# One loop step of a six-layer windowed-attention kernel, issued in another order: the transposes of a step stand together between the two halves of the scores

## The reference, cut to what matters

```python
for i in range(DEPTH):                     # 6
    x = attn_layer(shift_tokens(x), Wqkv[i], q_scale[i], k_scale[i], Wo[i]) + x
    x = ffn_layer(shift_tokens(x), ln_g[i], ln_b[i], W1[i], b1[i], W2[i], b2[i]) + x
# attn_layer: q, k, v = split(x @ Wqkv) in 16 heads of 64; q, k = l2norm, scale, rotary
#   (a rotary table times xPos scale); attention of each window of 32 tokens to itself and the
#   window before, softmax(8 * q k^T + mask) v; then @ Wo
# ffn_layer: layer norm, hg = xn @ W1 + b1 (2 x 341 wide), (a * gelu(gate)) @ W2 + b2
```

## Time and profile before

| | |
|---|---|
| median of 3 runs | 1505.93 us (1504.41 to 1509.35) |
| profiled execution | 1507.59 us, span of its trace 1505.8 us |
| busy, share of the span | TensorE 96%, VectorE 88%, ScalarE 77%, GpSimd 80% |
| chain that ended last | TensorE 89%, VectorE 5%, issue 2%, GpSimd 2% |

### The profile page before, as it was taken

One profiled execution on the slowest core, in us unless ns is written; L12 is line 12 of the kernel. 1 busy time (PEld: TensorE's weight loads), 2 busy tenths in 40 slices (PEclk: granted clock), 3 DMA queues, 4 the chain that ended last, 5 costly groups with the idle time before them and its releaser, 6 DMA issues.

```text
span 1505.8 us, 74802 instructions
## 1 busy us (share of the span) xinstructions
PE 1441.7 (96%) x32904; PEld 785.9 (52%) x32904; DVE 1327.1 (88%) x1789; ACT 1162.2 (77%) x2289; POOL 1209.8 (80%) x1051
## 2 busy tenths in 40 slices
PE   6877999999999999999999999999999999999985
PEld 6823444545545545545545545545555545545553
DVE  5478999989999989999999999989999999999974
ACT  4337888878888788888888888888888788888871
POOL 5148999878888888888888888888888888888841
PEclk9968999999999999999999999999999999999998
DMA  5100000020000020000020000020000000000000
GB/s 206 30 1 30 3 10 10 3 66 10 4 20 15 4 66 10 3 20 15 3 66 10 4 19 15 4 66 10 3 20 15 4 10 10 4 20 15 4 17 29
DMA packets 24564, 32.93 MB, mean 22 GB/s; under 512 B 2372, under 2 KB 21424, under 8 KB 23344
## 3 DMA queue, kind: packets, MB, share of 16 engines
q1 hardware_dynamic: 24240, 28.15, 5.8%
HBM read 20.80 MB, written 1.05 MB: 15 GB/s over the span
## 4 chain that ended last, share of the span: by engine, by line
PE 89%; DVE 5%; issue 2%; POOL 2%; ACT 1%; DMA 1%; SPq 0%; POOLq 0%; DVEq 0%; ACTq 0%
PE psq L257 22%; PE ring L279 21%; PE ring L309 11%; PE pss L298 9%; PE ring L267 9%; PE ring L323 8%; PE ring L333 4%; PE ring L346 1%; DVE qa L825 1%; PE ring L382 1%; DVE qb L841 1%; DVE mx L983 1%; DVE qb L961 1%; DMA xf<-x 0%; DMA mh<-in_bv 0%
## 5 line engine op out<-in xcount | busy, mean ns | idle before, releaser
L279 PE MATMUL ring<-mh,x0S 128*32 128x512 f32 x3072 | 407.9, 595 | 0.0
L257 PE MATMUL psq<-wqk,x0S 128*32 128x512 f32 x3072 | 394.9, 612 | 5.9 <-ACT sq L1200 4.9
L1332 POOL TENSOR_TENSOR qa<-qa,qb 128x1024 f32<-128x1024 f32 x96 | 229.2, 2388 | 6.7 <-DVE qb L961 6.7
L1391 POOL TENSOR_TENSOR qa<-qa,qb 128x1024 f32<-128x1024 f32 x96 | 228.6, 2382 | 0.0
L309 PEld LDWEIGHTS ring<-u,pT 128*32 128x32 f32 x6144 | 171.4, 111 | 61.8 <-issue 60.1
L309 PE MATMUL ring<-u,pT 128*32 128x128 f32 x6144 | 191.6, 274 | 4.1 <-DVE pT L978 4.1
L1373 POOL TENSOR_TENSOR pr<-pr,rden 128x1024 f32<-128x1024 f32 x96 | 183.9, 1916 | 12.8 <-DVE rden L860 12.8
L257 PEld LDWEIGHTS psq<-wqk,x0S 128*32 128x32 f32 x3072 | 93.6, 111 | 184.2 <-issue 168.4
L1352 POOL TENSOR_TENSOR qa<-qa,rn 128x1024 f32<-128x1024 f32 x96 | 182.7, 1903 | 0.2
L1368 POOL TENSOR_TENSOR qa<-qa,rn 128x1024 f32<-128x1024 f32 x96 | 182.8, 1904 | 0.0
L298 PEld LDWEIGHTS pss<-kT,qT 64*32 64x32 f32 x12288 | 134.8, 105 | 91.1 <-issue 83.6
(11 more groups left out here) (172 smaller groups left out, 2724.3 us busy)
## 6 DMA issues: line engine op xcount, KB each, us to landing
wqk<-in_wqk SPq DMA_DIRECT2D x6, 1024.0 KB, 8.6
mvT<-in_mvT SPq DMA_DIRECT2D x6, 512.0 KB, 3.8
wo<-in_wo SPq DMA_DIRECT2D x6, 512.0 KB, 5.2
xf<-x SPq DMA_DIRECT2D x24, 128.0 KB
xf<-x SPq DMA_DIRECT2D x24, 127.0 KB
rope<-in_rope SPq DMA_DIRECT2D x1, 2048.0 KB, 10.0
w<-in_w SPq DMA_DIRECT2D x6, 341.0 KB, 3.0
xmid<-in_x SPq DMA_DIRECT2D x4, 256.0 KB, 4.2
```

The lines of the kernel that those rows point to most:

```text
L257: last = mm(psq[WIN * w:WIN * w + WIN, 512 * (n % 2):512 * (n % 2) + 512], x0S[:, tile * P + WIN * w:tile * P + WIN * w + WIN], wqk[:, l % ...
L279: last = mm(bank[WIN * g:WIN * g + WIN, :], x0S[:, tile * P + WIN * w:tile * P + WIN * w + WIN], mh[:, l % 2, g, :, :].rearrange("p j n -> ...
L1332: g_.tensor_tensor(qa[:, t % 2, 1024:2048], qa[:, t % 2, 1024:2048], qb[:, 1024:2048], ALU.add).then_inc(sum_k, 1)
L1391: g_.tensor_tensor(qa[:, t % 2, 0:1024], qa[:, t % 2, 0:1024], qb[:, 0:1024], ALU.add).then_inc(sum_q, 1)
```

## The change

The instructions are the same, in number and form; each engine issues them in another order and with other lags.

TensorE after: H, Y part 1 (t=s-6), A2, A0, U1, U0 (s-4), K(s-1), S0(s-4), T01(s-3), T23(s-3), S1(s-4), U3(s-5), F, G0, U2(s-4), G1, A1, Z, Q(s-1), X, G2, Y part 0 (s-5). By s mod 4: F in 0; H, G0, G1 in 1; A0, A1, G2 in 2; A2, Z, X in 3.

VectorE after: L961, L983, L978, A1 (L834), statistics (L895), L816, Z (L929), L825, L841, Y (L851), L867, L956, L936, L969, A2 (L906), A0 (L876), L857, L860, L947. ScalarE after: T2 and T3 copies, L1124, U3, G0, L1157 to L1163, xh, U2, G2, X, F0, G1, F1, L1204, L1200, the exponential (L1176), U0, H, U1, L1254, L1129 and L1133, T0 and T1 copies. G0 and G1 stand ahead of the exponential of one step, G2 ahead of that of the next. GpSimd after: L1346, L1332, L1336, L1338, L1368, L1352, the group's norm, L1391, L1373, L1328. (Numbers are those of the lines before.) The chunks of the first part and the last group's norm move with them: the first K now stands in step 1 behind chunks 4, 5 and 6.

The diff of TensorE's loop, cut to the guards and the calls (waits and bank bookkeeping are left out and go with their calls):

```diff
@@ -506,89 +506,41 @@
+i = group_at(s, 9)
+        merge((j, j + 1), l)
-i = group_at(s, 14)
-    hidden(ring[bank], 2, 1).then_inc(filled[bank], 1)
-t = s - 5
-    values(ring[bank], t, 3).then_inc(filled[bank], 1)
-t = s - 4
-    values(ring[bank], t, 2).then_inc(filled[bank], 1)
-t = s - 4
-    scores(t, 1).then_inc(s_ready, 1)
-t = s - 3
-    turn([ring[bank] for bank, n in banks], t, 0)
-t = s - 1
-    project(t, 0)
-    project(t, 1).then_inc(pq_done, 1)
-i = group_at(s, 14)
-    hidden(ring[bank], 1, 0).then_inc(filled[bank], 1)
-i = group_at(s, 12)
-    halves_turned([ring[bank] for bank, n in banks], lambda blk: xh[:, blk * P:blk * P + P], QUAD)
-t = s - 5
-    mix(ring[bank], t, 0)
-i = group_at(s, 13)
-    hidden(ring[bank], 0, 1).then_inc(filled[bank], 1)
-u = unit_at(s, 3)
-t = s - 5
+t = s - 6
     mix(ring[bank], t, 1).then_inc(filled[bank], 1)
-i = group_at(s, 13)
+i = group_at(s, 15)
+    hidden(ring[bank], 2, 0).then_inc(filled[bank], 1)
+i = group_at(s, 14)
     hidden(ring[bank], 0, 0).then_inc(filled[bank], 1)
-t = s - 3
+t = s - 4
+    values(ring[bank], t, 1).then_inc(filled[bank], 1)
+t = s - 4
@@ -597,42 +549,7 @@
     values(ring[bank], t, 0).then_inc(filled[bank], 1)
-i = group_at(s, 15)
-    narrow(ring[bank]).then_inc(filled[bank], 1)
-i = group_at(s, 14)
-    hidden(ring[bank], 2, 0).then_inc(filled[bank], 1)
-t = s - 3
-    values(ring[bank], t, 1).then_inc(filled[bank], 1)
-i = group_at(s, 8)
-        merge((j, j + 1), l)
-i = group_at(s, 13)
-    hidden(ring[bank], 1, 1).then_inc(filled[bank], 1)
-t = s - 0
+t = s - 1
@@ -648,6 +565,94 @@
     project(t, 2)
     project(t, 3).then_inc(pk_done, 1)
+t = s - 4
+    scores(t, 0)
+t = s - 3
+    turn([ring[bank] for bank, n in banks], t, 8)
+t = s - 3
+    turn([ring[bank] for bank, n in banks], t, 0)
+t = s - 4
+    scores(t, 1).then_inc(s_ready, 1)
+t = s - 5
+    values(ring[bank], t, 3).then_inc(filled[bank], 1)
+u = unit_at(s, 3)
+i = group_at(s, 12)
+    halves_turned([ring[bank] for bank, n in banks], lambda blk: xh[:, blk * P:blk * P + P], QUAD)
+i = group_at(s, 13)
+    hidden(ring[bank], 0, 1).then_inc(filled[bank], 1)
+t = s - 4
+    values(ring[bank], t, 2).then_inc(filled[bank], 1)
+i = group_at(s, 13)
+    hidden(ring[bank], 1, 1).then_inc(filled[bank], 1)
+i = group_at(s, 14)
+    hidden(ring[bank], 1, 0).then_inc(filled[bank], 1)
+i = group_at(s, 15)
+    narrow(ring[bank]).then_inc(filled[bank], 1)
+t = s - 1
+    project(t, 0)
+    project(t, 1).then_inc(pq_done, 1)
 i = group_at(s, 15)
@@ -658,24 +663,19 @@
     halves_turned([ring[bank] for bank, n in banks], lambda blk: x0T[:, QUAD * (i % GROUPS) + blk, :], QUAD)
-t = s - 2
-    turn([ring[bank] for bank, n in banks], t, 8)
-t = s - 3
-    scores(t, 0)
+i = group_at(s, 14)
+    hidden(ring[bank], 2, 1).then_inc(filled[bank], 1)
+t = s - 5
+    mix(ring[bank], t, 0)
```

And of ScalarE's, the blocks around the gates and the exponential:

```diff
+                i = group_at(s, 13)
...
+                    nc.scalar.activation(uT[0:rows, 0, :], ring[bank][0:rows, :], ACT.Gelu,
...
+                i = group_at(s, 14)
...
+                    nc.scalar.activation(uT[0:rows, 2, :], ring[bank][0:rows, :], ACT.Gelu,
...
+                i = group_at(s, 13)
...
+                    nc.scalar.activation(uT[0:rows, 1, :], ring[bank][0:rows, :], ACT.Gelu,
...
+                t = s - 4
+                if 0 <= t < STEPS:
+                    act.wait_ge(p_shifted, t + 1)
+                    nc.scalar.activation(pr[:, t % 2, :], pr[:, t % 2, :], ACT.Exp, scale=QK_SCALE).then_inc(exp_done, 1)
```

More of the change, by code:

```diff
@@ L557, in _ @@
-                t = s - 5
[L558 to L563, removed]
-                    mix(ring[bank], t, 0)
-                i = group_at(s, 13)
[L566 to L570, removed]
-                    if i % GROUPS == 0:
-                        pe.wait_ge(w1_ready, 16 * (i // GROUPS + 1))
-                    wait(pe, freed[bank], n)
-                    hidden(ring[bank], 0, 1).then_inc(filled[bank], 1)
@@ L650, in _ @@
                     project(t, 3).then_inc(pk_done, 1)
+                t = s - 4
+                if 0 <= t < STEPS:
+                    if t == 0:
+                        mask(t)
+                    wait(pe, mask_ready, t)
+                    bank, n = place["T1", t]
+                    pe.wait_ge(freed[bank], n + 1)
+                    bank, n = place["T3", t]
+                    pe.wait_ge(freed[bank], n + 1)
+                    pe.wait_ge(kprev_ready, t + 1)
+                    scores(t, 0)
@@ new lines, in _ @@
+                if chunk_at(s - 1, 3) >= 0:
+                    chain_d(chunk_at(s - 1, 3))
+                i = group_at(s, 13)
+                if i >= 0:
+                    bank, n = take("G0", i)
+                    for r in range(2):
+                        nbank, m = place["F%d" % r, i]
+                        pe.wait_ge(freed[nbank], m + 1)
+                    if i % GROUPS == 0:
+                        pe.wait_ge(w1_ready, 16 * (i // GROUPS + 1))
+                    wait(pe, freed[bank], n)
+                    hidden(ring[bank], 0, 1).then_inc(filled[bank], 1)
@@ L826, in _ @@
                                     tab[:, t % 2, 0, :].unsqueeze(1).broadcast_to([P, HEADS, HD]), ALU.mult)
[L827 to L837 removed]
+                if chunk_at(s, 0) >= 0:
+                    chain_W(chunk_at(s, 0))
                 t = s - 1
@@ new lines, in _ @@
+                i = group_at(s, 8)
+                if 0 <= i < LASTG:
+                    l, first = i // GROUPS + 1, i % GROUPS
+                    for j in ((first, first + 1) if first % 2 == 0 else ()):
+                        bank, n = place["H%d" % j, l]
+                        act.wait_ge(filled[bank], n + 1)
+                        nc.scalar.copy(mh[:, l % 2, :, 2 * (j % 2) + j // 2, :],
+                                       ring[bank][:, :].rearrange("p (k n) -> p k n", k=4)).then_inc(freed[bank], 1)
```

699 lines of the change are left out of this document (337 added, 362 removed).

## The result

The kernel after takes 1521.17 us (median of 4 runs, 1519.28 to 1522.56), the kernel before beside it 1506.78 (4 runs): a ratio of 1.0094 with a 95% interval of 1.0074 to 1.0115. The change costs 14 us, where I had forecast 1508.2 with a range of 1490 to 1530. The profiled execution took 1520.87 us, its span is 1518.8, 13.0 above the span before.

What follows compares the result with a forecast made beforehand. TensorE's blocks from start to start were taken as the bound. Terms -24 (blocks), +5 (X alone), +19.3 (psq loop), +2 (start and end) gave +2.3 us: 1508.2 against a median of 1505.93, range 1490 to 1530.

Steps and rivals of the forecast that it cites:

- TensorE's blocks: TensorE's steps: leaving the wide tiling once instead of twice saves 0.25 us a step, -24 us over 96 steps.
- The rival in which nothing is saved: TensorE's tiling cost belongs to the matmuls' modelled ends, so the blocks give nothing: 1527 us, chance 0.03.
- The loop through psq: K and Q share one buffer; TensorE waits for VectorE and ScalarE between them, +19.3 us.
- some 20: Sign: TensorE waits for L1124 before Q and L1200 before K, classes 0 and 3, some 20 us in all.
- the rival in which the waits don't come: The psq waits are a third of those forecast and TensorE keeps its saving: 1495 us, chance 0.25.
- ScalarE's tables: Four table loads a group instead of two on ScalarE, 62 us in all, expected hidden and taken as nothing.
- Start and end: Filling and emptying of the pipeline: +2 us together, from -4 to +8.
- K(3) some 2 us later: Start: the chunk chain ends some 3 us earlier, but K(3) comes some 2 us later, +2.
- The steps without group work: The seven steps without group work take 12.7 us each for 12.39, +2 us.
- the end: The last K stands half a step nearer to the last scores, -2 us.
- the open table load: Rival: a ScalarE load delays the next L947 and Q in classes 1 and 2: 1532 us, chance 0.18.
- my own case: Gains and waits cancel: 1508.2 us, own range 1500 to 1517, chance 0.52.

Runs made afterwards that it cites:

- e6: Kernel after with a third buffer for the rotated queries and keys and each squaring on ScalarE cut into halves: 1498.66 us, ratio 0.9944 to the kernel before.
- e2: Kernel after with a third buffer for the rotated queries and keys: 1508.93 us, ratio 1.0013 to the kernel before.
- e1: Kernel after with chunks 5 to 15 of the first part one loop step later, K(0) again ahead of chunk 5: 1520.46 us.
- e3: Kernel after with T01 back ahead of S0 (order K, T01, S0, T23, S1): 1557.22 us, ratio 1.0335 to the kernel before.
- e9: Kernel after with third buffer and halved squarings, plus 128 already met waits in TensorE's stream ahead of the loop: 1505.11 us.
- e10: Kernel after with third buffer and halved squarings, U3 moved between the transposes and S1: 1558.28 us, ratio 1.0345 to the kernel before.
- e4: Kernel after with the gates' gelu replaced by the identity, so no table switches in the loop: 1517.79 us, ratio 1.0079 to the kernel before.
- e5: Kernel after with each squaring on ScalarE cut into two of 512 columns: 1510.73 us, ratio 1.0028 to the kernel before.
- e12: Kernel after with third buffer and halved squarings, ScalarE's copies of X moved behind the mask: 1497.32 us, ratio 0.9940 to the kernel before.

## Why the prediction was right or wrong

**TensorE's blocks: right.** Each block took what it was given, and e6, where nothing else binds, shows the group 0.84 us shorter than before without H and 0.85 with it, for a forecast of 0.75. The rival in which nothing is saved falls.

**The loop through psq: right in mechanism and size.** From tile 12 to 95 the blocks should have given 83 x 0.25 - 17 x 0.25 = 16.5 us. The loop took 4.9 longer, of which 3.3 are new gaps (below), so 18.1 us went into it; the forecast's 19.3 for all 96 steps is 16.7 for these. Undisturbed groups came out at +0.34 and -0.23 for +0.23 and -0.19. By the starts of K and Q, a group without H stands behind that of e6 by 0.17 us before Q and 0.57 before K in class 0 (forecast 0.18 and 0.49) and by 0.44 in the other classes (0.31). It was not seen from the list of waits, where the psq waits make 6.4 us for the "some 20" that I had named as the sign, just the figure of the rival in which the waits don't come: as e2 shows, the list has only what goes beyond a block's modelled end, and a short wait not at all. Two edits that only shorten this loop gave 22.5 us together in the kernel after, 15.3 of them between tiles 12 and 95, and 1 to 2 in the one before.

**ScalarE's tables: right.** I took nothing, and 3.4 us is the most they cost. The load hides in a wait for another engine: each starts 17 to 19 ns behind the end of ScalarE's instruction ahead of it, whatever the one that needs it still waits for. The Trainium skill, "ScalarE: Activation LUTs", section "What ACT_TABLE_LOAD costs", adds draining of about 1380 ns to a switch; each of the 44 exponentials behind a load starts 11 to 12 ns after the load's end, so that no run here shows the draining, ahead of a load or behind it.

**Start and end: this is the step that failed.** It was given +2 (from -4 to +8) and measured +8.1: +8.5 up to tile 12 and -0.4 at the end. Of its three terms "K(3) some 2 us later" is the one that was wrong: K(3) comes 7.3 us later and K(4) 6.5. The steps without group work added the 2.0 that they were given, and the end gave back 0.4 for 2. I had found that the chain of chunks ends some 3 us earlier; it ends 1.8 earlier (its last L444 starts at 123.95, before at 125.73), but the first K and Q don't follow it. K(0) starts 5.4 us later behind its links, and Q(0) and Q(1) stand behind links that wait for VectorE. I had not put the first part's layer norms into that walk either: between 60 and 200 us TensorE waits 11.8 us for psq where it waited 3.6 (and 0.4 for another copy), and the longest, 4.33 us, is K(3)'s behind L1023 and L760. In e6, with the loop shortened, K(12) still comes at 248.80 for 244.69, 4.1 us late. How the 6.5 us divide between the chain's place and the layer norms isn't shown: e1 shows only that K(0)'s place alone isn't the cause, and an order that moves the layer norms out of K(3)'s way wasn't tried.

**Not in the sum at all: the gaps in TensorE's stream.** They make 8.7 us in 11 places for 5.4 in 3 before, +3.3. The waits of the kernel before had two lines of them, which I passed over:

```profile
PE ring L267 <- issue: 3.0, 2, 2.0
PE pss L298 <- issue: 2.4, 1, 2.4
```

By the profile's page, queue 8 brings 4.24 MB in 259 packets of 16 KB; TensorE's 65,808 instructions (matmuls and loads) make 64 bytes each if all of it is theirs, so one packet is some 256 instructions. In e3's gap the packet came here (DMA view from 611.30 to 611.40 us; queue, packets, MB, share):

```profile
q8 instruction: 1, 0.02, 54.9%
```

and TensorE went on at 613.74, 2.4 us later; the gaps that end at 951.88 in the kernel after and at 309.33 in the one before have their packets 2.9 and 2.5 us ahead. In the new order 160 short matmuls, 320 instructions, run from 608.12 to 610.83, 2.71 us, so that 256 are through in 2.2. In the old order at most 88 stand together (X, T01 and S0), with 16 wide ones behind. The Trainium skill, "Runtime: NRT & Kernel Launch", section "Instruction fetch mechanics", names the same blocks of 256 instructions and holds that crossing one is mostly hidden; in this run of short matmuls it isn't. e9 and e10 bear the mechanism out: the gaps move with the stream, and go when the run is broken up. So does a count: number TensorE's matmuls, loads and semaphore instructions through in the order of each trace, and all 135 gaps between 200 and 1434 us of the fourteen traces, the three of the kernel before among them, stand at remainder 192, 193 or 194 of 256. The kernel after passes 225 such places. At nine of them 149 or more matmuls of the run are through, and each of the nine has a gap; of the other 216 two have one. Why e3, with as long a run, has 29 of them for 11, many at places where the kernel after has none, and why the kernel before has three at all, stays open.

**The verdict.** The forecast sum of +2.3 us was 10.7 short of the span's +13.0: 6.1 in start and end, 3.3 in the gaps, 1.3 over all the rest. So the outcome that my sum gave, within 0.3%, did not come, and "slower by over 0.3%" did. I had given it 0.37, the most of the three, but 0.18 of that was the open table load, which e4 rules out, and only 0.14 my own case: that the sign was foreseen at all is luck. The time lies in the range of 1490 to 1530, but above my own case's 1500 to 1517, and by none of the rivals' mechanisms.

## What to carry to other kernels

A block set ahead of another delays the readers on the other engines by its whole length. Before TensorE's saving is booked, walk each single-buffered tile round its loop (writer, readers in their engines' order, next writer) and compare that with the work that stands between; here one more buffer and a squaring in two halves turned a loss of 0.9% into a gain of 0.6%, and gave the old order nothing that its interval tells from no change (ratio 0.9991, 0.9976 to 1.0007). Walk the pipeline's filling with every engine's set-up work in it, not only with the chain that looks longest, and don't pack several hundred short instructions on TensorE into under 3 us without looking at its gaps.

## What the runs showed of the hardware

- A run of 160 short matmuls (320 instructions in 2.71 us) meets gaps of 0.2 to 1.6 us named "issue", which end 2.2 to 3.0 us behind a 16 KB packet of queue 8. Ten of them stand at the same matmuls in seven kernels (after, e1, e2, e4, e5, e6, e12). They move by 32 matmuls when 64 instructions are put ahead (e9) and vanish when a wide block parts the run (e10), and in every kernel that has them they stand a multiple of 256 instructions apart, to within 2.
- 16 transposes between halves of the scores cost 0.64 us, 32 in one piece 1.14: there is a price of 0.14 us a step for changing between the forms 64\*128 and 64\*32 twice more (e3).
- A table load of 1.28 us cost next to nothing where its engine would have waited: 89 of them, 114 us of ScalarE, were worth 3.4 us (e4). No draining shows: 17 to 19 ns ahead of a load, 11 to 12 between it and the exponential.
- A wait in front of a matmul shows only in part as idle time, since the modelled end of the block ahead reaches over it: K started 0.34 us late, and 0.16 of that stood in the list (e2).
